# Another order of the pieces on all engines of a four-layer sequence kernel, in the repeated turn and in a lead-up two turns longer

## The chip, the cores and the metric

The kernel runs on one core of one Trainium2 chip. The metric is the time of one execution on the device, in microseconds; lower is better. Three executions of the kernel before took 4561.04 to 4562.57 us, with a median of 4562.22 us.

## The reference

Input x has 32 batches of 256 positions with 256 features. Four layers follow one another, each with a residual; cut to what matters, and without biases and norm weights:

```python
# layer 0 (16 heads) and layer 3 (8 heads): linear attention
q = softmax(norm(x) @ Wq, over the features of a head)
k = softmax(norm(x) @ Wk, over the positions)
y = q @ (k.T @ v)
x = x + silu(norm(y) * (1 + scale(cond)) + shift(cond)) @ Wo
# layer 1 (16 heads): full softmax attention
y = softmax(q @ k.T, over the keys) @ v           # then as above
# layer 2: conditioned selective scan, E = 512, N = 16, once forward and once backward
delta = softplus(u @ Wdbc @ Wdt)
h[t]  = exp(delta[t] * A) * h[t-1] + delta[t] * B[t] * u[t]     # (E, N) numbers per position
y[t]  = sum over N of h[t] * C[t]  +  u[t] * Dp
x = x + gate * ((silu(mx) * (y_forward + y_backward)) @ Wf + skip)
```

## The kernel before, in words

`bass_kernel` (L1610) allocates everything, sets up the weights of layers 0, 1 and 3 (`setup_weights`, L1042), and then starts one instruction stream on each engine with `program` (L1519). The kernel is a software pipeline over the 32 batches: while one batch is in the scans, later ones are in layers 0 and 1 and in the front of layer 2, and an earlier one is in layer 3.

The work of an engine is cut into strands, one for each letter, and each strand is a generator whose `yield`s cut it into pieces. Between the pieces of one strand the order is fixed; between strands it is set by tables of letters alone. `program` runs the pieces in the order of `FIRST[engine]` (L1481, the lead-up), and then repeats `TURN[engine]` (L1497, the repeated turn, one batch of every strand); a letter whose strand is over is skipped. Every wait is written in the piece that needs it, so the tables decide only how early or late a piece stands, and what is queued behind it when it waits. The letters:

- W: weights of the scan layer, made once (on DVE `w_dve`, L1286, lines L1295 to L1371).
- L: layer 0. On DVE the maxima of q and k (L245 to L251), the reciprocals (L254 to L261), y (L265) and the new x (L279); on POOL the product L342.
- A: layer 1. On DVE eight reductions over the scores (`A_sm`, L428; m0 to m7 here), the reciprocal L433, the new x (L279); on POOL the product L484.
- C: the front of layer 2. POOL does m1 and m2 (L656, L659). For each of the two directions DVE makes the delta, `C_dd`, from two inputs in SBUF (L572; d0 and d1 here), POOL multiplies it into delta times u (L663, du0 and du1, which waits for d0 or d1) and writes a column that stops the carry (L665). The result goes to DRAM and comes back as `S_slot`. L668 is the gate.
- S: the scans. A batch has 32 units in 4 columns of 8: four of the forward direction, then four of the backward one. For each unit POOL makes the product with B (L758, S0 to S31), ACT the exponentials in two halves (L699), DVE two scans (L714, S0.0, S0.1 and so on), and PE sums over the states (L793).
- P: the product of the scanned states with C. Units 1, 3, ... 29 have it on POOL (L771, P1, P3, ...), the others on DVE in two halves (L729, P0.0, P0.1, ...).
- G: the gating on DVE (L741), once in a column.
- T: layer 3, with the projection that closes layer 2. It runs the lines of L, and in front of them L821 (`T.gated`) and L824 (`T.x`, which has two inputs in SBUF and makes the x that layer 3 starts from).

Two rings bound how far the engines may part. The exponentials and scans use three PSUM banks, so the exponential of a half waits for what frees the bank three halves before (the scan where P is on POOL, P where it is on DVE). The products with B use eight buffers, so S of a unit on POOL waits for the sum of the unit eight before.

```python
            if i == 0:
                v.wait_ge(S.b.sem, S.b.at(b, "%d" % u))
            v.wait_ge(S.exp.sem, S.exp.at(b, "%d_%d" % (u, i)))
```

```python
        g.wait_ge(S.dve.sem, S.dve.at(b, "d%d" % s))
        g.tensor_tensor(B["dd"][:, :, 1, :], B["dd"][:, :, 1, :], B["dd"][:, :, 0, :], ALU.mult).then_inc(S.pool.sem, 1)
```

The first of these is the start of a scan half (L710 to L712), the second du0 and du1 (L662, L663).

Of the kernel before, what the change touches and what calls it, by code (L numbers as in the profile page):

```python
# [1479 lines left out]

FIRST = {  # L1481
    "PE": (
        "WWWWWWWWWWWWWWWLLLLWLWWWWWLWWLWWWWWWWWWWWWWLWWWWWWLWWWWWWWWWWWWWLAAAAAAAAAAAAAAAAAAAAAAAAAALALLLALLLLLLAAAAAAACACACACACA"
        "ACAAAAACAAAACAACAACCLALLCLALLLLLCLSASAAAAASACSASCACSACACAACASSASASSASSACASASAACASSSACASASCSSCSSSLALSLSCLALSLSSLSSLSLCSSS"
        "LSTASAAAAASACSASCACSATC"),
    "DVE": (
        "WWWWLWWWWWWWWWWWWWWWLWLWWWWLWLWWWWWWWWWWWWWWWWWLWWWWWWWWWWWWWWLWLWWWWWWWWWWWWWWWWWWWWWWWLWAWWWAAAAAAAAAAALLLLLLLLALACCAA"
        "AAAAAACAAALLLLLLCLLASPSLPASSSCPSPSSCSPSSPASASASPASPASASPASASSPGSCPSPSSSPSPSSSSPPSSSPSPSSSSPPSSGSSAPAPSASLSPSSPSLLSSPLSPS"
        "SSLPSPGSSSPSLPC"),
    "ACT": (  # L1490
        "LLLWLLLLLLLLLLAAAAAAAAAAAAAAAAAAALLAAALALLLLLLLLLLAACAAACAACCCCCCCACCAAAACAAACAAACCALLACAALALLLLLCCCCLLLLLSSCSCSCCSASACA"
        "SSSASASCAASCSSCCSSCCSSSSCCACSCSSASSASSASSASSCASASSSASCASSSASSSACSSCSSALSLSACSASALSASLSSSLLSSLSLSCCCCSSSS"),
    "Pool": "LALCCCACSLSSSCPCCSSPSSPSSSSPSSPCSPSSSSPPSSSSSPPPSSSPSSAPSPSC",
    "SP": "LAWWALACCCACLssCCACssCSSCASCLSStSssCCACss",
}
# [177 lines left out]
```

## Time and profile before

| what | value |
|---|---|
| median of 3 executions | 4562.22 us (4561.04 to 4562.57) |
| profiled execution, its span | 4567.5 us |
| DVE busy | 4075.3 us, 89% of the span |
| POOL busy | 3933.3 us, 86% |
| PE busy | 3809.5 us, 83% |
| ACT busy | 3679.7 us, 81% |

The profiled execution is one of its own, beside the three that were timed; of it the span alone is known, which is 5.3 us (0.12%) above their median. Times inside the trace count from the start of that span. A busy share is a mean over the lead-up, some 28 turns alike, and the end, so it does not say which engine sets the length of a turn; that is read from one turn.

### The profile page before, as it was taken

The page shows a single profiled execution, that of the slowest core. Times are in us where ns is not written, and L with a number is a line of the kernel's source. Part 1 is how long each engine was busy: PE and PEld are TensorE (multiplying, and loading weights), DVE is VectorE, ACT ScalarE, POOL GpSimd, SP SyncE. Part 2 cuts the span into 40 slices and gives each one's busy share as a digit, 9 for nine tenths or more (in the row PEclk, how much of TensorE's full clock was granted, in tenths as well). Part 3 has the DMA queues.
Part 4 walks back from the last instruction along what each step waited for, and adds up shares of the span by engine and source line. Part 5 has one row for each costly group of instructions (what it writes and reads, how often), then busy time and mean ns, then how long its engine had stood idle before and what let it go on. Part 6 is the DMA issues. An engine that isn't in the chain of part 4 may idle for free.

```text
span 4567.5 us, 73193 instructions
## 1 busy us (share of the span) xinstructions
PE 3809.5 (83%) x26068; PEld 2509.1 (55%) x26068; DVE 4075.3 (89%) x5552; ACT 3679.7 (81%) x8678; POOL 3933.3 (86%) x1836
## 2 busy tenths in 40 slices
...
GB/s 124 1 8 63 86 108 114 114 116 104 125 115 116 104 97 116 116 116 109 111 118 120 110 93 112 116 112 117 104 124 115 116 103 101 117 113 113 113 108 36
DMA packets 338584, 470.58 MB, mean 103 GB/s; under 512 B 56474, under 2 KB 166149, under 8 KB 338217
## 3 DMA queue, kind: packets, MB, share of 16 engines
...
## 4 chain that ended last, share of the span: by engine, by line
ACT 28%; DVE 22%; POOL 21%; PE 21%; issue 6%; DMA 1%; SPq 1%; DVEq 0%; POOLq 0%; ACTq 0%
POOL S_X L758 13%; ACT ps L699 11%; PE ps L170 8%; POOL S_X L771 6%; DVE S_X L714 5%; PE ps L375 5%; DVE ps L714 5%; DVE A_sm L428 4%; DVE S_X L729 3%; PE ps L394 2%; PE ps L793 2%; PE ps L160 1%; POOL C_dd L663 1%; ACT wa L633 1%; ACT A_ring L153 1%
## 5 line engine op out<-in xcount | busy, mean ns | idle before, releaser
L758 POOL TENSOR_TENSOR S_X<-S_slot,S_bc 128x1024 f32<-128x1024 f32 x1024 | 2398.3, 2368 | 18.6 <-PE ps L793 9.4
L699 ACT ACTIVATE ps<-S_slot,acol 128x256 f32<-128x256 f32 x4096 | 1728.2, 468 | 203.3 <-DVE S_X L729 192.9
L714 DVE TENSOR_TENSOR_SCAN ps<-ps,S_X 128x512 f32<-128x512 f32 x1088 | 1301.1, 1214 | 26.2 <-ACT ps L699 16.0
L714 DVE TENSOR_TENSOR_SCAN S_X<-ps,S_X 128x512 f32<-128x512 f32 x960 | 1138.0, 1206 | 28.5 <-ACT ps L699 26.6
L771 POOL TENSOR_TENSOR S_X<-S_X,S_bc 128x1024 f32<-128x1024 f32 x480 | 1133.4, 2366 | 34.1 <-DVE S_X L714 32.0
L729 DVE TENSOR_TENSOR S_X<-ps,S_bc 128x512 f32<-128x512 f32 x1088 | 723.5, 672 | 10.4
L793 PE MATMUL ps<-S_X,sum 128*32 128x256 f32 x8192 | 621.2, 406 | 83.7 <-POOL S_X L771 73.2
L394 PE MATMUL ps<-A_qP,A_kP 32*128 32x256 f32 x2048 | 318.0, 431 | 123.8 <-ACT A_ring L471 64.1
L793 PEld LDWEIGHTS ps<-S_X,sum 128*32 128x32 f32 x8192 | 201.3, 112 | 371.4 <-issue 175.2
L428 DVE TENSOR_REDUCE A_sm<-ps 128x4 f32<-128x1024 f32 x256 | 312.2, 1220 | 91.0 <-PE ps L375 81.0
L375 PE MATMUL ps<-A_kP,A_qP 32*128 32x256 f32 x2048 | 301.3, 413 | 46.9 <-DVE A_sm L428 26.2
L394 PEld LDWEIGHTS ps<-A_qP,A_kP 32*128 32x128 f32 x2048 | 191.0, 198 | 229.4 <-ACT A_ring L471 105.5
L471 ACT ACTIVATE A_ring<-ps 128x1024 f32<-128x1024 f32 x256 | 259.0, 1012 | 49.7 <-PE ps L394 49.6
L170 PE MATMUL ps<-C_xT,wcz 128*128 128x256 f32 x1024 | 289.8, 433 | 1.0 <-ACT C_dd L609 0.9
L342 POOL TENSOR_TENSOR T_ke<-T_ke,T_xh 128x512 f32<-128x512 f32 x64 | 82.2, 1284 | 233.7 <-ACT T_xh L335 233.7
L663 POOL TENSOR_TENSOR C_dd<-C_dd 128x1024 f32<-128x1024 f32 x64 | 150.9, 2359 | 144.4 <-DVE C_dd L572 144.4
L375 PEld LDWEIGHTS ps<-A_kP,A_qP 32*128 32x128 f32 x2048 | 180.6, 190 | 164.3 <-DVE A_sm L428 91.7
L160 PE MATMUL ps<-ident,T_q 128*128 128x128 f32 x512 | 108.8, 349 | 167.5 <-ACT T_q L153 161.3
L170 PEld LDWEIGHTS ps<-C_xT,wcz 128*128 128x128 f32 x1024 | 214.1, 220 | 57.5 <-issue 24.9
L160 PEld LDWEIGHTS ps<-ident,T_q 128*128 128x128 f32 x512 | 69.4, 172 | 217.7 <-ACT T_q L153 177.3
L484 POOL TENSOR_TENSOR A_ring<-A_ring 128x512 f32<-128x512 f32 x32 | 40.9, 1279 | 170.4 <-ACT A_ring L335 170.4
L785 PE MATMUL ps<-C_xT,wD 128*128 128x256 f32 x512 | 147.7, 413 | 40.7 <-DVE S_g L741 39.8
...
## 6 DMA issues: line engine op xcount, KB each, us to landing
S_slot<-scr_dd SPq DMA_DIRECT2D x1024, 256.0 KB, 4.6
...
S_bc<-scr_bc SPq DMA_DIRECT2D x256, 256.0 KB, 6.3
...
```

The costliest lines, as they stand in the source:

```text
L160: ins = p.transpose(bank[:, col * 256 + r * P:col * 256 + (r + 1) * P], src[:, r, col * P:(col + 1) * P], ident[:])
L170: ins = p.matmul(out, l, r, start=n == 0, stop=n == len(terms) - 1)
L375: ins = p.matmul(bank[o][:, t * 256:(t + 1) * 256], B["qP"][r, g, t * P:(t + 1) * P], B["kP"][r, g, :], start=True, stop=True, tile_positi ...
L394: ins = p.matmul(bank[o][:, t * 256:(t + 1) * 256], B["kP"][r, g, t * P:(t + 1) * P], B["qP"][r, g, :], start=True, stop=True, tile_positi ...
L428: v.tensor_reduce(B["sm"][:, :, 2 * n:2 * n + 2].rearrange("p t h -> p h t"), B["pair"].rearrange("p h (t m) -> p h t m", t=TT), AX, ALU.m ...
L471: a.activation(B["ring"][:, 2 * (n % 4):2 * (n % 4) + 2, :], B["pair"], ACT.Exp).then_inc(S.act.sem, 1)
L699: ins = a.activation(B["bank"][half_at(b, u, i)][:, n * T:(n + 1) * T], B["slot"][:, s, j, 0, :], ACT.Exp, scale=K.k["acol"][:, s, LINES * ...
L714: v.tensor_tensor_scan(line(x if u in ON_POOL else decay), line(decay), line(x), 0.0, ALU.mult, ALU.add).then_inc(S.scan.sem, 1)
L729: v.tensor_tensor(B["X"][:, u % RING, 2 * i:2 * i + 2, :], state, rep(B["bc"][:, s, NQ + q, :], 1, 2), ALU.mult).then_inc(S.cv.sem, 1)
L758: g.tensor_tensor(B["X"][:, u % RING], B["slot"][:, s, :, 1, :], rep(B["bc"][:, s, q, :], 1, LINES), ALU.mult).then_inc(S.b.sem, 1)
L771: g.tensor_tensor(B["X"][:, u % RING], B["X"][:, u % RING], rep(B["bc"][:, s, NQ + q, :], 1, LINES), ALU.mult).then_inc(S.cp.sem, 1)
L793: ins = p.matmul(B["sums"][32 * j:32 * j + 32, (c % 2) * T:(c % 2 + 1) * T], K.k["sum4"][:], B["X"][:, u % RING, j, :], start=False, stop= ...
```

## The change

The tables `FIRST` and `TURN` are written anew for all five engines. Each `TURN` holds as many pieces of every letter as before. Each `FIRST` is longer by exactly two turns' pieces (on DVE 533 letters for 255, on POOL 170 for 60), so the pipeline stands at the same depth where the repeated turn begins. No instruction, wait, buffer or size changes. The lines behind the tables have numbers higher by 14. Of the diff the tables of POOL stand for all:

```diff
 FIRST = {
...
-    "Pool": "LALCCCACSLSSSCPCCSSPSSPSSSSPSSPCSPSSSSPPSSSSSPPPSSSPSSAPSPSC",
...
+    "Pool": (
+        "LALCCCSSSCPSALSSSSCSCCPSPPSSSSSSPPSCPSSSPSSPPSSPSPSSSSPSPSSAPCSLSSPSSSPCSCCSPSSSPSSSPPSSSCPSPSSSSPSTSSPPPSSSSPSPSCSP"
+        "SSASLSCPSSCCSPSSSSSPPPSSSPSPSSSCPSSSSPSTPPSSSPSSSPCAPS"
+    ),
...
 TURN = {
...
-    "Pool": "SPSLSSSCPCCSSPSSPSSSSPSSPCSPSSSSPPSSSSSPTPPSSSPSSAPSPSC",
...
+    "Pool": "SPSLSSSCPCCSSPSPSSSSSSPSPSSCSPPSSPSSSPSTSPSSPSPSAPSSPSC",
```

**POOL, second column of the scans.** Before, with S8 to S11, P7, S12, S13, P9, then du0 and its column (L663, L665), then S14 and P11:

```order
L758 TENSOR_TENSOR S_X<-S_slot,S_bc 128x1024 x4
L771 TENSOR_TENSOR S_X<-S_X,S_bc 128x1024
L758 TENSOR_TENSOR S_X<-S_slot,S_bc 128x1024 x2
L771 TENSOR_TENSOR S_X<-S_X,S_bc 128x1024
L663 TENSOR_TENSOR C_dd<-C_dd 128x4x256
L665 MEMSET C_dd 128x4
L758 TENSOR_TENSOR S_X<-S_slot,S_bc 128x1024
L771 TENSOR_TENSOR S_X<-S_X,S_bc 128x1024
```

Now, with S7 to S12, P7, S13, P9, then S14 and S15, and du0 behind them:

```order
L758 TENSOR_TENSOR S_X<-S_slot,S_bc 128x1024 x6
L771 TENSOR_TENSOR S_X<-S_X,S_bc 128x1024
L758 TENSOR_TENSOR S_X<-S_slot,S_bc 128x1024
L771 TENSOR_TENSOR S_X<-S_X,S_bc 128x1024
L758 TENSOR_TENSOR S_X<-S_slot,S_bc 128x1024 x2
L663 TENSOR_TENSOR C_dd<-C_dd 128x4x256
L665 MEMSET C_dd 128x4
```

Two products with B that stood behind du0 now stand between P9 and du0.

**DVE, the same place.** Before, from S9.0 and S9.1 to P10.1; d0 is L572, T's maximum of k is L251:

```order
L714 SCALAR_TENSOR_TENSOR S_X<-ps,S_X 128x512 x2
L729 TENSOR_TENSOR S_X<-ps,S_bc 128x512
L251 TENSOR_REDUCE T_km<-ps 128x2
L741 SCALAR_TENSOR_TENSOR S_g<-ps,bD,wa 128x256
L714 SCALAR_TENSOR_TENSOR ps<-ps,S_X 128x512
L572 SCALAR_TENSOR_TENSOR C_dd<-C_dd,C_tmp 128x4x256
L729 TENSOR_TENSOR S_X<-ps,S_bc 128x512
L714 SCALAR_TENSOR_TENSOR ps<-ps,S_X 128x512
L729 TENSOR_TENSOR S_X<-ps,S_bc 128x512
```

Now, from P8.1 ahead of S9.0 to P10.1:

```order
L729 TENSOR_TENSOR S_X<-ps,S_bc 128x512
L714 SCALAR_TENSOR_TENSOR S_X<-ps,S_X 128x512 x2
L714 SCALAR_TENSOR_TENSOR ps<-ps,S_X 128x512
L741 SCALAR_TENSOR_TENSOR S_g<-ps,bD,wa 128x256
L729 TENSOR_TENSOR S_X<-ps,S_bc 128x512
L714 SCALAR_TENSOR_TENSOR ps<-ps,S_X 128x512
L572 SCALAR_TENSOR_TENSOR C_dd<-C_dd,C_tmp 128x4x256
L251 TENSOR_REDUCE T_km<-ps 128x2
L729 TENSOR_TENSOR S_X<-ps,S_bc 128x512
```

P8.1 moved ahead of S9.0, S10.1 and P10.0 ahead of d0, the maximum of k behind it; and P10.1 no longer follows at once on the scan whose result it reads.

**DVE in the lead-up.** Before, around the end of batch 0's layer 1 and the start of batch 1's layer 0, with none of the W work left:

```order
L433 RECIPROCAL A_srec<-ps 128x32
L436 TENSOR_TENSOR A_qP<-ps,A_srec 128x512
L135 BN_STATS A_raw<-A_qP 128x6 x2
L138 BN_AGGR A_mv<-A_raw 128x2 x2
L135 BN_STATS T_raw<-L_xin 128x6 x2
L138 BN_AGGR T_mv<-T_raw 128x2 x2
L245 TENSOR_REDUCE T_qm<-ps 128x32
```

Now batch 1's layer 0 is at its end while W's pieces (L1295 to L1299) still run between its own:

```order
L259 SCALAR_TENSOR_TENSOR T_bd<-ps,same 128x128 x2
L261 RECIPROCAL T_qm<-ps 128x32
L1299 COPY wdt<-ps 64x512
L1297 TENSOR_SCALAR wcz<-ps,S_bc 128x512
L265 TENSOR_TENSOR T_q<-ps,T_qm 128x512
L135 BN_STATS T_raw<-T_q 128x6 x2
L138 BN_AGGR T_mv<-T_raw 128x2 x2
L1297 TENSOR_SCALAR wcz<-ps,S_bc 128x512
L1299 COPY S_slot<-ps 128x256 x3
L279 TENSOR_TENSOR A_x<-ps,A_x 128x512
L279 TENSOR_TENSOR A_x<-ps,L_xin 128x512
```

Layer 0 of batch 1 moved from behind the W work to between its pieces, and with it the start of batch 1's layer 1.

## Rows read from the trace of the kernel before

**Rows 1.** The page's first part: busy time, share of the span, instructions.
```profile
PE 3809.5 (83%) x26068; PEld 2509.1 (55%) x26068; DVE 4075.3 (89%) x5552; ACT 3679.7 (81%) x8678; POOL 3933.3 (86%) x1836
```
**Rows 2.** Stretches: us, busy PE, PEld, DVE, ACT, POOL, granted clock, DMA share, GB/s.
```profile
200.00:300.00 100.00, 62.47 (x307) 38.70 (x306) 14.93 (x22) 24.48 (x47) 1.26 (x1) 0.62 0.01 3
...
3107.00:3234.00 127.00, 111.38 (x802) 73.87 (x802) 124.25 (x169) 114.42 (x271) 123.03 (x58) 0.96 0.48 112
...
3361.00:3490.00 129.00, 113.75 (x801) 74.78 (x800) 124.36 (x168) 114.55 (x271) 122.64 (x58) 0.93 0.48 111
```
**Rows 3.** The chain that ended last, one mark of each turn: start, us, what.
```profile
2596.20 2.47 ACT ps L699 x6
...
2725.28 2.47 ACT ps L699 x6
...
2852.12 2.47 ACT ps L699 x6
...
4127.90 2.47 ACT ps L699 x6
```
**Rows 4.** Waits of DVE, 600 to 4200 us: total, times, longest.
```profile
DVE S_X L714 <- ACT ps L699: 16.6, 28, 1.9
```
**Rows 5.** Waits of POOL, the same stretch.
```profile
POOL C_dd L663 <- DVE C_dd L572: 80.9, 56, 1.7
```
**Rows 6.** POOL's timeline at du0: start, us, engine, line, [idle before].
```profile
3171.75 4.77 POOL L758 TENSOR_TENSOR S_X<-S_slot,S_bc 128x1024 f32<-128x1024 f32 x2
3177.16 2.36 POOL L771 TENSOR_TENSOR S_X<-S_X,S_bc 128x1024 f32<-128x1024 f32 x1 [0.64 <-DVE S_X L714]
3181.10 2.37 POOL L663 TENSOR_TENSOR C_dd<-C_dd 128x1024 f32<-128x1024 f32 x1 [1.58 <-DVE C_dd L572]
```
**Rows 7.** DVE's timeline of the same turn, from one d1 to the next.
```profile
3119.71 1.23 DVE L572 SCALAR_TENSOR_TENSOR C_dd<-C_dd,C_tmp 128x1024 f32<-128x1024 f32 x1
...
3174.76 2.32 DVE L714 TENSOR_TENSOR_SCAN S_X<-ps,S_X 128x512 f32<-128x512 f32 x2
...
3179.81 1.21 DVE L572 SCALAR_TENSOR_TENSOR C_dd<-C_dd,C_tmp 128x1024 f32<-128x1024 f32 x1
...
3181.53 1.22 DVE L714 TENSOR_TENSOR_SCAN ps<-ps,S_X 128x512 f32<-128x512 f32 x1
3182.79 0.69 DVE L729 TENSOR_TENSOR S_X<-ps,S_bc 128x512 f32<-128x512 f32 x1
...
3246.55 1.22 DVE L572 SCALAR_TENSOR_TENSOR C_dd<-C_dd,C_tmp 128x1024 f32<-128x1024 f32 x1
```
**Rows 8.** DVE's timeline near the end, two L572.
```profile
4264.15 3.98 DVE L572 SCALAR_TENSOR_TENSOR C_dd<-C_dd,C_tmp 128x1024 f32<-128x1024 f32 x1
...
4320.51 5.20 DVE L572 SCALAR_TENSOR_TENSOR C_dd<-C_dd,C_tmp 128x1024 f32<-128x1024 f32 x1
```
**Rows 9.** POOL's timeline beside these two.
```profile
4262.31 2.42 POOL L771 TENSOR_TENSOR S_X<-S_X,S_bc 128x1024 f32<-128x1024 f32 x1
4264.65 2.40 POOL L758 TENSOR_TENSOR S_X<-S_slot,S_bc 128x1024 f32<-128x1024 f32 x1
...
4322.26 2.37 POOL L771 TENSOR_TENSOR S_X<-S_X,S_bc 128x1024 f32<-128x1024 f32 x1
```
**Rows 10.** DVE's timeline at one T.x.
```profile
3014.46 1.03 DVE L824 TENSOR_TENSOR xs<-T_x,T_xh 128x512 f32<-128x512 f32 x1
```
**Rows 11.** POOL's timeline beside it.
```profile
3012.59 2.35 POOL L771 TENSOR_TENSOR S_X<-S_X,S_bc 128x1024 f32<-128x1024 f32 x1
3015.09 1.53 POOL L656 TENSOR_TENSOR xs<-C_xh,C_mod 128x512 f32<-128x512 f32 x1
```
**Rows 12.** DVE's timeline in the lead-up, batch 1 and batch 2 leaving layer 0.
```profile
276.87 0.73 DVE L135 BATCH_NORM_STATS2 T_raw<-L_xin 128x6 f32<-128x256 f32 x2
...
316.75 0.69 DVE L279 TENSOR_TENSOR A_x<-ps,L_xin 128x512 f32<-128x512 f32 x1 [11.57 <-PE ps L170]
...
448.74 0.69 DVE L279 TENSOR_TENSOR A_x<-ps,L_xin 128x512 f32<-128x512 f32 x1 [1.39 <-PE ps L170]
```

More of the change, by code:

```diff
@@ L1482 @@
     "PE": (
-        "WWWWWWWWWWWWWWWLLLLWLWWWWWLWWLWWWWWWWWWWWWWLWWWWWWLWWWWWWWWWWWWWLAAAAAAAAAAAAAAAAAAAAAAAAAALALLLALLLLLLAAAAAAACACACACACA"
-        "ACAAAAACAAAACAACAACCLALLCLALLLLLCLSASAAAAASACSASCACSACACAACASSASASSASSACASASAACASSSACASASCSSCSSSLALSLSCLALSLSSLSSLSLCSSS"
-        "LSTASAAAAASACSASCACSATC"),
-    "DVE": (
-        "WWWWLWWWWWWWWWWWWWWWLWLWWWWLWLWWWWWWWWWWWWWWWWWLWWWWWWWWWWWWWWLWLWWWWWWWWWWWWWWWWWWWWWWWLWAWWWAAAAAAAAAAALLLLLLLLALACCAA"
-        "AAAAAACAAALLLLLLCLLASPSLPASSSCPSPSSCSPSSPASASASPASPASASPASASSPGSCPSPSSSPSPSSSSPPSSSPSPSSSSPPSSGSSAPAPSASLSPSSPSLLSSPLSPS"
-        "SSLPSPGSSSPSLPC"),
@@ L1490 @@
-    "ACT": (
-        "LLLWLLLLLLLLLLAAAAAAAAAAAAAAAAAAALLAAALALLLLLLLLLLAACAAACAACCCCCCCACCAAAACAAACAAACCALLACAALALLLLLCCCCLLLLLSSCSCSCCSASACA"
-        "SSSASASCAASCSSCCSSCCSSSSCCACSCSSASSASSASSASSCASASSSASCASSSASSSACSSCSSALSLSACSASALSASLSSSLLSSLSLSCCCCSSSS"),
-    "Pool": "LALCCCACSLSSSCPCCSSPSSPSSSSPSSPCSPSSSSPPSSSSSPPPSSSPSSAPSPSC",
-    "SP": "LAWWALACCCACLssCCACssCSSCASCLSStSssCCACss",
+        "WWWWWWWWWWLLWLLWWLLWLLWWLWWWWWWLWWAAAAAAWAWAWLAWAWALAWWAWWAAWLWAWAWWWWAALAWWALWALAALAAWLAWWWLWAWLWWWWWAWAAACAACACACA"
@@ new lines @@
+        "CACAALCAAALACACALAACAALACASCALALLCALLSALAAAAAASSASACSASCSCACAACASCSLSAASCLSSSAASASACLAACASSASSASSCSACSASSLLALSSSSLSC"
+        "LASSLSCSLSTAASAAAAATATSSASCSSACSACATSATCTACTACSSASTSASAASSATCASSCSTSAASCATASCLSCLASSLSSCSALSCSLLSSLSLLSSSASLTASAAASA"
+        "TTASACSACACTSSSASCAACATATSACSTSCSASASTAASAASSATACCTASSATSCSSSACLSLLSCLSASLSSLLASSLLCSSSSLTASAAAAASCSASSACTACSAC"
+    ),
+    "DVE": (
+        "WWWWWWWWLWLLWWWWWWLWWWWLWWWWWWWWLWLLWWWWWWWWWWWWWLAWLWWAWAAAWAWWAALWWWLAWWWWWLWWWWLWWWAAALWWLLWWWWALWCWWAWWWWWWWWWCW"
+        "WWALAAAAACAALLLSSPPSLSCAAASPSLPLSLASLASSPPSCSSPLSPSSSCPAASPASSASASAPSGAPSSASPCSLPSSSPSPLSSSPPSSLSSPSPSSGPSSPSSSPPSSS"
+        "SPALAPGSACSSPSSSPSPSPLSSLLSPSSPAPSPCGSPLSASPSSTPTSPSSTSSPASSPACTSATSPPASASSATPSPSSASGASPSPSSSCPPSSSSPSTPSSTSSPPTSTSG"
+        "PSPSSSPSSPSSTLSPSPSSPSPLLASASASGLSPPLSSSCPSPSSLSPLSLSPSPSPPSSGPASSLCPASPSSSPTTTSPSSCSPSTTPSSASSAPSSPATSSAPSAPAGSASPA"
+        "SPSSSSSPPSSCSPTPSSSSPTGPTTSSSPSSPSTSLSPSPASALLSPLASPLSSGCSSPPSSLSPSSP"
+    ),
@@ new lines @@
+    "ACT": (
+        "LLLLLLLLLLLLLAAALAAAALWAAALLAALLALAAALAAAAAALALLLLCAAACACAAACCLCCCCCCALCALCACASAASSALSASCALCCACCLALSLSCASACAACCLALLL"
+        "SLSCASASSASSACASSASACLCSSCCSCSSCSCSCLSCACSSSSASSASASCASSLCSSALSASSSSACSASSACSSSSACCSCSCLSALSSLASSALSSSAASCSLSLLSLSLS"
+        "SCCCSASASSACSSAASTAASCTSSCSCSSSCSTTSSCTSTCSCSASCTCSSCCSASSSASASSSSASSASSCTSASTATSCTTSASSSSACLSCSSLSCASCCSSCLALCSSLSL"
+        "SLSALSSACSSAASCLSSLLSLLSSCCSSSASACSASSATSSTASASCASSCCSSSTSCSSTCSSCTSTSASCSCTSACSSACSASASSASSASACSACTSTTTATSCSSSSACLS"
+        "LCCSCCSSLSLASLLASALSLASACSSSSSSS"
+    ),
@@ L1495 @@
+    "Pool": (
+        "LALCCCSSSCPSALSSSSCSCCPSPPSSSSSSPPSCPSSSPSSPPSSPSPSSSSPSPSSAPCSLSSPSSSPCSCCSPSSSPSSSPPSSSCPSPSSSSPSTSSPPPSSSSPSPSCSP"
+        "SSASLSCPSSCCSPSSSSSPPPSSSPSPSSSCPSSSSPSTPPSSSPSSSPCAPS"
+    ),
+    "SP": "LWAWLAACLCCCAssCCssASCLCSCSACSSCSssCCAtCssSSCASSCSLCSssCTstsACSLCCSSASCSSsstTACCCss",
 }
 TURN = {
-    "PE": "ACATACASSATSASSASSTACTASASTATATCASSSATCASASCSTSCSSSLALSLSCLALSLSSLSSLSLCSSSLSTASAAAAASACSASCACSATC",
+    "PE": "ATACACAASTSSCSASATASASTASTATATCASSSSATCAASCTSCSSASLSLSSCLSSLSALSLSLSLSLCSSSLTASAAAAASCASCASSTACSAC",
```

10 lines of the change are left out of this document (5 added, 5 removed).

## The prediction

> **What bounds the kernel now.** The page's first part shows that no engine is idle for long: DVE is busy 89% of the span, POOL 86%, PE 83%, ACT 81% [rows 1]. Such shares mix the lead-up with the turns, so I went to the table of stretches next. In a turn of 127 us DVE is busy for 124.25 and POOL for 123.03; DVE's spare time is some 2.75 us, POOL's 4 [rows 2]. Between 200 and 300 us it is the reverse: PE is busy for 62 us at a granted clock of 0.62, DVE for 15, and POOL does one instruction [rows 2]. So the kernel has two parts with different limits: a lead-up that waits for one batch to get through layers 0 and 1 on PE, and turns in which DVE and POOL have hardly a gap.
>
> The chain that ended last gives the length of a turn by its mark, six halves of exponentials: from 2596.20 to 4127.90 are 12 turns, 127.64 us each; a quick one takes 126.84 (2725.28 to 2852.12) [rows 3]. The slow turns are ones in which PE's clock falls once more, as in the stretch of 129 us at 0.93 beside that of 127 us at 0.96, with DVE busy for no longer (124.36 for 124.25) [rows 2].
>
> What DVE and POOL wait for tells where the order matters. POOL's largest wait is du0 and du1 for DVE's delta, 80.9 us in 56 waits, 1.4 us each [rows 5]; one of DVE's longest is of a scan for an exponential, 16.6 us in 28, a small sum [rows 4]. The first is a curious one. DVE's timeline has d0 start at 3179.81, the moment at which POOL has gone idle behind P9 (3177.16 + 2.36 = 3179.52) [rows 6, 7]. In a turn d0 and d1 thus fall into an empty POOL, and take 1.2 us. Near the end of the kernel they don't: there two of the same shape take 3.98 and 5.20 us [rows 8]. Beside the first, POOL's P ended at 4264.73, its next S began at 4264.65 in the record and ended at 4267.05, and DVE's instruction ended at 4268.13, 1.08 after that; beside the second, POOL's P ended at 4324.63, DVE at 4325.71, again 1.08 later [rows 8, 9]. **I read from this that DVE's L572 doesn't begin its work until POOL's queued instructions are through**, even where an instruction boundary lies between (4264.65), and that it then takes 1.1 to 1.2 us.
>
> **The change, part by part.** The counts of instructions don't change, so every term is a wait that goes or comes. I follow one turn from d1 to d1; before, d1 to d0 is 60.10 us (3119.71 to 3179.81) and d0 to d1 is 66.74 (to 3246.55), 126.84 in all [rows 7].
>
> *d1 to d0.* S9.1 ended 57.37 us after d1 (3174.76 + 2.32 - 3119.71) [rows 7]. Ahead of it one product more now stands (P8.1), +0.6, the distance of such a product to the next instruction. ACT does two halves of exponentials before the piece of layer 0 on which POOL's chain to S4 hangs: 2.47 / 6 = 0.41 each [rows 3], and as S4 has hardly any lead over its scan I charge +0.4. A scan with its product right behind costs 1.26 us from start to start (3181.53 to 3182.79 [rows 7]) where a scan before an independent instruction costs 1.16 (half of 2.32); ten of eleven such neighbours are parted in the new turn, and one lies in this stretch: -0.2 with what follows on it. Two of A's maxima are asked for earlier: +0.3, between 0 and 0.6. S9.1 then ends at 58.5.
>
> Now the step on which all rests. du0 now stands behind S14 and S15 on POOL. P9 waits for S9.1 as before (0.64 us of idle time [rows 6]), and then P9, S14 and S15 follow without a wait: 2.36 + 4.77 (the size of a pair of such products) = 7.1, less what the records overlap, 7.0 [rows 6]. DVE comes to d0 3.3 us after S9.1 (S10.0, the gating, P10.0, S10.1: 1.13 + 0.4 + 0.6 + 1.13), in the middle of S14. By the reading above it gets through only behind S15: its work starts at 58.5 + 7.0 = 65.5, and not at 61.8. Everything on DVE behind it stands still for 3.7 us, which DVE's 2.75 us of spare time do not cover, since they lie at other places.
>
> *d0 to d1.* Out go S10.1 and P10.0, -1.7; in comes the maximum of k, +0.6. Parted neighbours: -0.8 (seven at 0.1 to 0.13). POOL has T's product one scan unit earlier and a sum at S23 in time: -0.7, at most what DVE waits in a turn, 2.75, at least 0. That is 66.74 - 2.6 = 64.1. The maximum of k is 3.3 us later than before, and with it ACT's exponentials of layer 3's k, which lie between those of the scans: 0 to +1.0, I take +0.3. The turn becomes 65.5 + 64.4 = 129.9, +3.1 over the quick one; bounds +2.3 and +4. There are 28 turns in which d0 meets running scans (batches 4 to 31): **+87 us** (+64 to +112).
>
> *The lead-up.* Before, batch 1's layer 0 begins only after batch 0's layer 1 (276.87), and ends 40 us later (316.75) [rows 12], on an idle DVE. Now it is made between W's pieces, on a PE that W alone doesn't fill. I laid the new order of PE, ACT and DVE out with durations of the trace: batch 1's layer 1 starts at about 252 us (240 to 290), not 317. Batch 2 leaves layer 0 at 448.74 before [rows 12]; in the new order at about 374, 75 sooner, and with six scan halves more behind it, at 127.6 / 64 = 2.0 us each: 75 + 12 = 87, less some for their waits, 82. But in the lead-up too, L572 and L824 now fall beside a full POOL; by the same reading seven of them lose 1 to 4.7 us, 20 in all. **-62 us** (-90 to -40).
>
> *Nothing.* SP's new order moves loads that are needed tens of us later, with the same slots; at nothing, under the cover of the DMA engines' 48% share [rows 2]; if a slot came late, its S would wait, first on POOL. The end of the kernel drains in the same letters.
>
> **The sum.** 4567.5 + 87 - 62 = 4592.5 for a profiled span; less the 5.3 us by which that stands above the median, **4587 us**, +0.5%.
>
> **The rivals.**
>
> *DVE gets through at the next boundary.* At one L824, issued at 3014.46 beside P (3012.59 + 2.35 = 3014.94), the end was 3015.49, 0.55 after P's, and POOL's next, L656, took 1.53 [rows 10, 11]. So a boundary can be enough; but L656 waits for several semaphores, S15 for one. If it held for d0, it would start at S14's end, 58.5 + 4.7 = 63.2: a turn of 127.6, with POOL held up once +0.6 to +0.8 over the quick one; 28 x 0.6 = +17, the lead-up -72: 4562 - 55 = 4507. SBUF — State Buffer, of the Trainium skill, section "Who interferes with whom", states the rule that an instruction of DVE with two inputs in SBUF contends with GpSimd's reads, and that the order of issue decides who blocks for a whole instruction. By that rule this rival would be right, and the case below wrong; the trace agrees with the contention (3.98 and 5.20 us [rows 8]), but in the first of those POOL had two instructions in turn.
>
> *There is no such block.* The long L572 near the end would then have another cause, such as its own input. d0 starts at 61.8, the turn is 61.8 + 64.1 = 125.9, -0.9; 28 x -0.9 = -26, the lead-up -82: 4454. Against it: both long ones end 1.08 us behind a POOL instruction.
>
> *The block, and a lead-up that gives little* (the W pieces in turn delay layer 1 on PE), with T late for its full microsecond: 28 x 3.6 = +100, -40: 4622.
>
> *The block, and PE's clock falls once more in every turn*, since PE stands still with DVE: the slow turn before 2725.28 took 129.08 us, 2.2 over the quick one, where the mean is 0.8 over it [rows 3]; 28 x 1.4 = +40: 4627.
>
> **How the numbers follow.** My case has 0.50, the boundary 0.14, no block 0.12, the weak lead-up 0.14, the clock 0.10. About 0.2% (9 us) can be told from no change, so same is 4553 to 4571. Within my case the bounds of the turn (+64) and the lead-up (-90) reach 4536, and 0.06 of its 0.50 lie under 4553, 0.12 in between. Faster: 0.14 + 0.12 + 0.06 = 0.32. Same: 0.12. Slower: 0.32 + 0.14 + 0.10 = 0.56. The range leaves out the case without a block and a tail above the weak lead-up (4562 + 112 - 40 = 4634 at its bounds): 4495 to 4635. My case's own range is 4536 to 4634.
>
> **What would show it.** In the changed profile d0 (L572 at the second column) should last 4.5 to 4.9 us in each turn, d1 1.2; du0's wait for DVE, 1.6 us, should stay, behind S15; the marks of the chain should lie 129 to 131 us apart; the first L714 should stand near 370. d0 at 2.5 us and turns of 127.5 speak for the boundary, d0 at 1.2 for no block, and then I am wrong by over 1%. First L714 past 410 would break the lead-up's term.

## The result, and the profile after

The changed kernel takes 4579.09 us (median of 11 runs, 4565.88 to 4598.32), where the kernel before, in the same runs, takes 4562.22 us (4557.94 to 4571.9): 1.0041 times, 95% interval 1.0027 to 1.0056. It is slower by 17 us, where +25 was forecast. Its profiled execution has a span of 4589.5 us, 10 us above that median, so the trace shows a turn somewhat longer than the median execution has.

The first part of its page:

```profile
PE 3816.3 (83%) x26068; PEld 2500.9 (54%) x26068; DVE 4114.0 (90%) x5552; ACT 3667.2 (80%) x8678; POOL 3968.6 (86%) x1836
```

The shares are those of [rows 1]. DVE is busy for 39 us more and POOL for 35. On DVE the longer time is that of two lines alone: all L572 together last 139.5 us for 85.0, all L824 43.6 for 31.5, and no other line changes by 2 us. Both have two inputs in SBUF. (That is 67 us; busy time rises by less, since it counts once where two records overlap, and they overlap more in the new order.) On POOL the products with B (L758) last 26 us longer. Read beside the timelines below, this is time in which one engine stands in the way of the other. The table of stretches, to be read beside [rows 2]:

```profile
200.00:300.00 100.00, 88.56 (x491) 61.55 (x490) 31.51 (x65) 43.83 (x94) 7.84 (x6) 0.86 0.12 33
...
2304.00:2434.00 130.00, 112.91 (x808) 74.35 (x808) 125.00 (x169) 114.42 (x272) 124.38 (x58) 0.95 0.48 110
2434.00:2567.00 133.00, 115.10 (x805) 75.05 (x801) 126.92 (x168) 114.14 (x272) 124.14 (x58) 0.92 0.46 107
2567.00:2702.00 135.00, 117.55 (x808) 76.46 (x805) 127.13 (x169) 114.39 (x272) 124.98 (x58) 0.91 0.45 106
```

Between 200 and 300 us PE now is busy for 89 us at a granted clock of 0.86, where it was 62 at 0.62: the lead-up no longer waits for one batch. The turns are 130 to 135 us, and the long ones are those with the lower clock.

Where the time came from and went is told by the d1 of single batches (L572 on DVE, the second of each batch). Batch 4 and batch 31 in the changed kernel:

```profile
872.19 2.56 DVE L572 SCALAR_TENSOR_TENSOR C_dd<-C_dd,C_tmp 128x1024 f32<-128x1024 f32 x1
...
4400.52 2.37 DVE L572 SCALAR_TENSOR_TENSOR C_dd<-C_dd,C_tmp 128x1024 f32<-128x1024 f32 x1 [0.21 <-ACT C_tmp L625]
```

and in the kernel before:

```profile
949.84 1.23 DVE L572 SCALAR_TENSOR_TENSOR C_dd<-C_dd,C_tmp 128x1024 f32<-128x1024 f32 x1
...
4390.31 1.41 DVE L572 SCALAR_TENSOR_TENSOR C_dd<-C_dd,C_tmp 128x1024 f32<-128x1024 f32 x1
```

| part | before | after | difference |
|---|---|---|---|
| start to d1 of batch 4 | 949.8 | 872.2 | -77.7 |
| 27 turns, d1 of batch 4 to batch 31 | 3440.5 | 3528.3 | +87.9 |
| from there to the end | 177.2 | 189.0 | +11.8 |
| span | 4567.5 | 4589.5 | +22.0 |

That is 3.25 us for each of the 27 turns (the 22 us between the two profiled spans stand beside the 17 between the medians). DVE's waits between 600 and 4200 us, and then POOL's, beside [rows 4, 5] (us in total, times, longest):

```profile
DVE A_sm L428 <- PE ps L375: 41.6, 84, 2.4
DVE S_g L741 <- PE ps L793: 37.5, 31, 1.9
```

```profile
POOL S_X L758 <- PE ps L793: 54.1, 33, 3.2
...
POOL C_dd L663 <- DVE C_dd L572: 32.5, 28, 1.2
```

du0's wait for d0 is gone: the 28 waits that are left are those of du1. A new one has come, of POOL's product with B for a sum of PE. One turn shows how. PE's timeline at layer 1's last score product and its maxima:

```profile
2230.29 1.28 PE L375 MATMUL ps<-A_kP,A_qP 32*128 32x256 f32 x8
2232.90 0.39 PE L381 MATMUL ps<-ident,A_sm 128*16 128x128 f32 x2 [1.33 <-DVE A_sm L428]
2233.22 0.64 PE L793 MATMUL ps<-S_X,sum 128*32 128x256 f32 x8
```

DVE's:

```profile
2231.62 1.23 DVE L428 TENSOR_REDUCE A_sm<-ps 128x4 f32<-128x1024 f32 x1 [1.66 <-PE ps L375]
...
2238.75 0.48 DVE L741 SCALAR_TENSOR_TENSOR S_g<-ps,bD,wa 128x256 f32<-128x256 f32 x1 [1.94 <-PE ps L793]
...
2240.88 1.21 DVE L572 SCALAR_TENSOR_TENSOR C_dd<-C_dd,C_tmp 128x1024 f32<-128x1024 f32 x1
```

POOL's, with P7, S13, P9, the pair S14 and S15, and du0:

```profile
2228.96 2.34 POOL L771 TENSOR_TENSOR S_X<-S_X,S_bc 128x1024 f32<-128x1024 f32 x1
2233.97 2.36 POOL L758 TENSOR_TENSOR S_X<-S_slot,S_bc 128x1024 f32<-128x1024 f32 x1 [2.67 <-PE ps L793]
2236.28 2.37 POOL L771 TENSOR_TENSOR S_X<-S_X,S_bc 128x1024 f32<-128x1024 f32 x1
2238.60 5.69 POOL L758 TENSOR_TENSOR S_X<-S_slot,S_bc 128x1024 f32<-128x1024 f32 x2
2244.25 2.35 POOL L663 TENSOR_TENSOR C_dd<-C_dd 128x1024 f32<-128x1024 f32 x1
```

Two things are to be seen. PE's L381 waits for DVE's last maximum, and the sum of unit 5 (2233.22), which the new order puts behind it, comes late for POOL's S13, which stands idle for 2.67 us. And d0 starts at 2240.88, the moment at which S14 ends, takes 1.21 us, and it is POOL's S15 that is held up: the pair takes 5.69 us, where such a pair took 4.77 [rows 6]. d0 did not wait until POOL was through. Over batches 4 to 31 d0 lasts 1.2 us ten times, 1.5 to 1.8 eight times, 2.8 to 2.9 nine times and 2.55 once, and never the 4.5 to 4.9 that were forecast.

d1, for which 1.2 us were forecast, is held up too. DVE's and POOL's timelines at one of them:

```profile
2434.34 2.54 DVE L572 SCALAR_TENSOR_TENSOR C_dd<-C_dd,C_tmp 128x1024 f32<-128x1024 f32 x1
```

```profile
2433.43 2.36 POOL L758 TENSOR_TENSOR S_X<-S_slot,S_bc 128x1024 f32<-128x1024 f32 x1
2436.95 2.35 POOL L663 TENSOR_TENSOR C_dd<-C_dd 128x1024 f32<-128x1024 f32 x1 [1.16 <-DVE C_dd L572]
```

DVE now asks for d1 while POOL's last product in front of du1 runs, and d1 ends 1.09 us behind it. In the repeated turns of every kernel here with the new turn, whichever steps of it are undone below, d1 lasts 2.0 to 2.7 us; in all kernels with the old turn it lasts 1.2 to 1.3. In the changed kernel that is 33 us of DVE's time in 27 turns. No run takes it away, so what it costs the turn was not measured.

### The profile page after: what moved, and what is told of

It is laid out like the page before. It is cut to its first block, busy times and chain, and to the rows that moved or that the text cites. A ratio compares the mean times of both kernels' runs of the same rounds, so it can differ in the third digit from the quotient of the medians.

```text
span 4589.5 us, 73193 instructions
## 1 busy us (share of the span) xinstructions
PE 3816.3 (83%) x26068; PEld 2500.9 (54%) x26068; DVE 4114.0 (90%) x5552; ACT 3667.2 (80%) x8678; POOL 3968.6 (86%) x1836
## 4 chain that ended last, share of the span: by engine, by line
PE 37%; DVE 26%; ACT 21%; issue 8%; POOL 5%; DMA 1%; SPq 0%; DVEq 0%; POOLq 0%; ACTq 0%
PE ps L170 21%; ACT ps L699 8%; DVE ps L714 7%; DVE S_X L714 7%; PE ps L375 4%; DVE A_sm L428 4%; ACT A_ring L471 4%; PE ps L793 3%; DVE S_X L729 3%; POOL S_X L758 3%; PE ps L394 2%; PE ps L160 2%; ACT T_q L153 1%; POOL S_X L771 1%; ACT T_ke L325 1%
## 5 line engine op out<-in xcount | busy, mean ns | idle before, releaser
L758 POOL TENSOR_TENSOR S_X<-S_slot,S_bc 128x1024 f32<-128x1024 f32 x1024 | 2430.3, 2393 | 101.8 <-PE ps L793 61.3
L793 PE MATMUL ps<-S_X,sum 128*32 128x256 f32 x8192 | 633.2, 408 | 107.0 <-POOL S_X L771 93.9
L394 PE MATMUL ps<-A_qP,A_kP 32*128 32x256 f32 x2048 | 313.9, 427 | 44.2 <-ACT A_ring L471 39.4
L471 ACT ACTIVATE A_ring<-ps 128x1024 f32<-128x1024 f32 x256 | 260.1, 1016 | 94.3 <-PE ps L394 92.7
L170 PE MATMUL ps<-C_xT,wcz 128*128 128x256 f32 x1024 | 272.7, 413 | 3.1 <-ACT C_dd L609 2.8
L394 PEld LDWEIGHTS ps<-A_qP,A_kP 32*128 32x128 f32 x2048 | 187.9, 198 | 154.5 <-ACT A_ring L471 89.0
L160 PE MATMUL ps<-ident,T_q 128*128 128x128 f32 x512 | 99.6, 326 | 196.7 <-ACT T_q L153 190.9
L170 PEld LDWEIGHTS ps<-C_xT,wcz 128*128 128x128 f32 x1024 | 198.1, 204 | 66.2 <-issue 34.7
L663 POOL TENSOR_TENSOR C_dd<-C_dd 128x1024 f32<-128x1024 f32 x64 | 150.4, 2350 | 79.7 <-DVE C_dd L572 79.7
L609 ACT ACTIVATE C_dd<-ps,bdt 128x256 f32<-128x256 f32 x256 | 106.3, 467 | 141.1 <-PE ps L538 141.1
L538 PE MATMUL ps<-C_dbc,wdt 64*128 64x256 f32 x512 | 148.2, 411 | 41.2 <-ACT C_dd L615 41.1
```

Source lines behind the costliest of these rows:

```text
L160: ins = p.transpose(bank[:, col * 256 + r * P:col * 256 + (r + 1) * P], src[:, r, col * P:(col + 1) * P], ident[:])
L170: ins = p.matmul(out, l, r, start=n == 0, stop=n == len(terms) - 1)
L394: ins = p.matmul(bank[o][:, t * 256:(t + 1) * 256], B["kP"][r, g, t * P:(t + 1) * P], B["qP"][r, g, :], start=True, stop=True, tile_positi ...
L471: a.activation(B["ring"][:, 2 * (n % 4):2 * (n % 4) + 2, :], B["pair"], ACT.Exp).then_inc(S.act.sem, 1)
L758: g.tensor_tensor(B["X"][:, u % RING], B["slot"][:, s, :, 1, :], rep(B["bc"][:, s, q, :], 1, LINES), ALU.mult).then_inc(S.b.sem, 1)
L793: ins = p.matmul(B["sums"][32 * j:32 * j + 32, (c % 2) * T:(c % 2 + 1) * T], K.k["sum4"][:], B["X"][:, u % RING, j, :], start=False, stop= ...
```

## The experiments

Eleven variants, in four groups. All times are medians, and each ratio is to the kernel before in the same runs. That kernel's median lay between 4562 and 4571 us from one set of runs to the next, so a difference between variants of different sets is good to some 8 us, unless it is taken over the ratios.

**The lead-up and the turn apart.** Both tables come whole from one kernel and whole from the other, which is possible since the pipeline stands at the same depth where the turn begins.

```diff
 # the changed kernel, with TURN of before (first) or with FIRST of before (second)
-TURN = {...}     # changed
+TURN = {...}     # before
...
-FIRST = {...}    # changed
+FIRST = {...}    # before
```

> The lead-up of the change with the repeated turn of before. In the changed kernel's trace batch 4 passes d1 78 us earlier than before (872.19 for 949.84 us), and each later turn loses 3.2. If lead-up and turn are independent, the 78 us stay and turns are 127.6 us: 4562 - 78 = 4484. If the gain of the lead-up only exists because the engines stand further apart than the old turn lets them (so that the first turns give it back), it is 4520 or more. The last two turns inside the new lead-up already have the new order's waits and cost some 6 us of it in both.

> The lead-up of before with the repeated turn of the change. Independent parts: every turn from the end of the old lead-up 3.2 us longer, 28 to 30 times, and 12 us more in the drain at the end, where the changed kernel took 189.0 us behind its last d1 for 177.2: 4562 + 94 + 12 = 4668. If the loss in the turns comes from the state that the new lead-up leaves behind, and not from the turn's order, under 4600.

The new lead-up with the old turn takes 4505.11 us, ratio 0.9863 (0.9847 to 0.9879): 60 us faster, and the fastest kernel of this study. The old lead-up with the new turn takes 4660.54 us, 1.0207 (1.0185 to 1.0229): 96 us slower. The signs of the two halves are settled: the lead-up gains, the turn loses. In the first of the two the d1 of batches 4 and 31 are:

```profile
886.45 1.25 DVE L572 SCALAR_TENSOR_TENSOR C_dd<-C_dd,C_tmp 128x1024 f32<-128x1024 f32 x1
...
4327.36 1.40 DVE L572 SCALAR_TENSOR_TENSOR C_dd<-C_dd,C_tmp 128x1024 f32<-128x1024 f32 x1
```

63 us ahead of the kernel before, at both: the 27 turns between take 3440.9 us, as before (3440.5). Of the 78 us that the lead-up had gained where the new turn follows, 14 were given back where the old one takes over. The expectation, 4484, was too low by 21 us: by these 14, by the 3 that the kernel before took more here (4565.02), and by 4 that stay open.

**One step of the change in the kernel before.** First POOL's alone, du0 behind S14 and S15 (S15 comes in front of P11 by it too):

```diff
-    "Pool": "SPSLSSSCPCCSSPSSPSSSSPSSPCSPSSSSPPSSSSSPTPPSSSPSSAPSPSC",
+    "Pool": "SPSLSSSCPCCSSPSSPSSSSPSSPSSCPSSSPPSSSSSPTPPSSSPSSAPSPSC",
```

> The kernel before with one step of the change on POOL alone: in the repeated turn the products for units 14 and 15 stand in front of du0. DVE reaches d0 2.7 us behind S9.1, during the first of them. If d0 has to wait until POOL's queue is through (the prediction), it lasts 5.5 us in each turn and 28 x 4 = 112 us are added: 4675. If it gets in at the next boundary of POOL's instructions, it lasts 3.2 us, POOL's second product is held up by 1.1, and 28 x (1 to 2) are added: 4590 to 4620. If there is no contention d0 stays at 1.2 and the time at 4562.

4627.3 us, 1.0142 (1.0126 to 1.0157). DVE's d0 and POOL's pair and du0 in one of its turns:

```profile
2562.05 3.11 DVE L572 SCALAR_TENSOR_TENSOR C_dd<-C_dd,C_tmp 128x1024 f32<-128x1024 f32 x1
```

```profile
2561.71 5.66 POOL L758 TENSOR_TENSOR S_X<-S_slot,S_bc 128x1024 f32<-128x1024 f32 x2
2567.34 2.35 POOL L663 TENSOR_TENSOR C_dd<-C_dd 128x1024 f32<-128x1024 f32 x1
```

d0 is asked for beside S14, lasts 3.11 us and ends at 2565.16, 1.1 us behind the end of S14 (2561.71 + 2.35); S15 is held up by 1.0. It gets in at the next boundary of POOL's instructions: not the block to the end of the queue that I had read, but the first rival. The price is +2.1 us a turn (129.7 for 127.6), 64 in all, which is just above the 2 that were the upper end for the boundary. Near the end of the same kernel it is otherwise again:

```profile
4371.27 9.72 DVE L572 SCALAR_TENSOR_TENSOR C_dd<-C_dd,C_tmp 128x1024 f32<-128x1024 f32 x1
```

```profile
4372.97 2.33 POOL L771 TENSOR_TENSOR S_X<-S_X,S_bc 128x1024 f32<-128x1024 f32 x1
4375.26 4.63 POOL L758 TENSOR_TENSOR S_X<-S_slot,S_bc 128x1024 f32<-128x1024 f32 x2
```

Here d0 ends at 4380.99, 1.1 us behind POOL's last queued product (4379.89), with three boundaries, at 4372.97, 4375.26 and inside the pair, gone by. So neither reading holds everywhere: in the turns the boundary lets d0 in, near the end it often does not.

Second PE's step alone, L381 in front of the sums of units 5 and 6:

```diff
-    "PE": "ACATACASSATSASSASSTACTASASTATATCASSSATCASASCSTSCSSSLALSLSCLALSLSSLSSLSLCSSSLSTASAAAAASACSASCACSATC",
+    "PE": "ACATACAASSTSASSASSTACTASASTATATCASSSATCASASCSTSCSSSLALSLSCLALSLSSLSSLSLCSSSLSTASAAAAASACSASCACSATC",
```

> The kernel before with one step of the change on PE alone: in the repeated turn the transposes of layer 1's maxima (L381), which wait for DVE's last maximum, stand in front of the sums of units 5 and 6. Theory PE: POOL then waits in each turn for the sum of unit 5, 1 to 2.7 us, and 28 times 1 to 2.5 are added: 4590 to 4630. If the wait is covered (POOL in this order asks for the sum of unit 5 one instruction earlier, but DVE's last maximum comes earlier too), under 4575.

4605.07 us, 1.0092 (1.0072 to 1.0112), +41. The wait is there in each turn, as in this one (PE's timeline, then POOL's):

```profile
2555.57 0.39 PE L381 MATMUL ps<-ident,A_sm 128*16 128x128 f32 x2 [1.42 <-DVE A_sm L428]
2555.88 1.07 PE L793 MATMUL ps<-S_X,sum 128*32 128x256 f32 x16
```

```profile
2556.63 2.36 POOL L758 TENSOR_TENSOR S_X<-S_slot,S_bc 128x1024 f32<-128x1024 f32 x1 [1.84 <-PE ps L793]
```

Both steps together (the two diffs above):

> The kernel before with both single steps of the change: on POOL the products for units 14 and 15 in front of du0 (alone +62 us), on PE L381 in front of the sums of units 5 and 6 (alone +41). If the two losses add, 4562 + 103 = 4665, the whole of what the new turn costs with the old lead-up (+96 us). If they cover each other, since both hold POOL and DVE at the same place of the turn, 4625 to 4640.

4614.39 us, 1.0103 (1.0082 to 1.0125): 43 us over before, less than the first step costs alone. The losses do not add. What the trace shows is that POOL waits for the sum in each turn here too, and that d0 now lasts 1.21 to 2.53 us instead of 3.1; that the one brings the other, by shifting POOL's queue against DVE, is a reading. And together they are not the whole: the new turn costs 96 with this lead-up, so more than half of it is not accounted for by these two. Two things that the other moves bring are in the traces and were not tried apart: d1's 2.0 to 2.7 us, which this kernel does not have (1.2 to 1.3), and the time that PE spends at the lower clock, of which more below.

**Steps undone in the changed kernel.** PE's step undone:

```diff
-    "PE": "ATACACAASTSSCSASATASASTASTATATCASSSSATCAASCTSCSSASLSLSSCLSSLSALSLSLSLSLCSSSLTASAAAAASCASCASSTACSAC",
+    "PE": "ATACACASSATSCSASATASASTASTATATCASSSSATCAASCTSCSSASLSLSSCLSSLSALSLSLSLSLCSSSLTASAAAAASCASCASSTACSAC",
```

> The changed kernel with one thing undone on PE in the repeated turn: the sums of units 5 and 6 stand in front of the transposes of layer 1's maxima (L381) again. Theory PE: POOL's product for unit 13 waits 2.67 us for the sum of unit 5, which stands on PE behind L381, which waits for DVE's last maximum; that is the turn's main loss, the wait goes under 0.5 us, turns shrink by 2 to 2.7 us, and the time is 4579 - 26 x 2.3 = 4520. Theory POOL (the prediction's): the loss comes from products with B queued in front of du0, and the turn keeps at least 129.3 us: 4570 or more; then with POOL free earlier, d0 should show as 3.5 us long in every turn instead of 1.2.

POOL's step undone:

```diff
-    "Pool": "SPSLSSSCPCCSSPSPSSSSSSPSPSSCSPPSSPSSSPSTSPSSPSPSAPSSPSC",
+    "Pool": "SPSLSSSCPCCSSPSPSSSSSSPSPCSSSPPSSPSSSPSTSPSSPSPSAPSSPSC",
```

> The changed kernel with one thing undone on POOL in the repeated turn: du0 (L663) stands directly behind P9 again, in front of the products for units 14 and 15. Theory POOL (the prediction's): d0 never waits for POOL again, turns shrink by over 2 us, to under 128.5, 4579 - 26 x 2.6 = 4511. Theory PE: d0 already begins at an instruction boundary of POOL in most turns (1.21 us in 12 of 27, up to 2.86 in the others), so at most 1 us a turn comes back: 4555 to 4579, and POOL's wait of 2.7 us for the sum of unit 5 stays.

The first takes 4549.39 us, 0.9961 (0.9948 to 0.9975), the second 4550.91 us, 0.9965 (0.9954 to 0.9975): 28 to 30 us less than the changed kernel, each. In the first POOL's wait for sums falls from 54.1 to 5.8 us, turns are 127.3 to 130.8, and d0 lasts 2.7 us in each. In the second nearly every turn is 129.7 us long and d0 takes 1.21, but du0 waits up to 3.5 us, 124.0 us in 55 waits, since DVE comes to d0 only behind S10.1. Each step gave part of the time back, and neither all that its theory had promised.

Both undone:

> The changed kernel with both steps undone: PE's sums of units 5 and 6 in front of L381, and POOL's du0 directly behind P9. Alone they gave -30 and -28 us. If the two losses are separate they add: 4579 - 58 = 4521. If they cover each other (either of them sets the turn), the second gives little more: 4540 to 4550. DVE still reaches d0 only behind S10.1, so POOL keeps a wait of up to 3.5 us at du0.

4626.04 us, 1.0127 (1.009 to 1.0164): not faster than one alone, but 77 us slower. Neither theory held. The trace shows where the time is. Between batches 4 and 29 fifteen of its turns take 129.7 to 130.8 us and ten take 134.7 to 136.2, with the same instructions, and d0 lasts 1.2 in all of them. The same place of a short turn and of the long one behind it, as stretches (the columns are those of [rows 2]), and DVE's wait, 600 to 4200 us:

```profile
2666.00:2683.00 17.00, 14.65 (x139) 10.22 (x138) 15.99 (x23) 16.90 (x40) 17.00 (x9) 1.00 0.36 84
2796.00:2813.00 17.00, 17.00 (x86) 11.34 (x84) 8.85 (x16) 9.98 (x24) 13.08 (x7) 0.50 0.29 64
```

```profile
DVE S_g L741 <- PE ps L793: 38.1, 10, 3.8
```

In the long turn PE's granted clock goes to the lower of its two levels (1.2 GHz, half of full speed) at 2796, after PE had waited 1.5 us for a product of POOL. For 17 us PE is busy throughout and makes 86 matmuls, where it made 139. The waits come behind that: POOL stands idle for 3.9 us for a sum up to 2809.27, DVE for 3.8 up to 2811.72, once in each of the ten long turns. So most of what this kernel loses is PE at half speed: ten turns that are 5.7 us longer make 57 us. Why the clock falls at this place in some turns and not in others is not shown; in the short turn PE waits as long there (1.46 us), and it does not fall.

And with d0 directly behind S10.0 on DVE as well:

```diff
-    "DVE": "LSLSAPSSPSPPSGPSLPACSSSTPSTPSSCTSSPSPASASAPSASPASSAPTATSAPSSSGPSCTPSSSSPTSPSSSPPSSTSPTSTSGPSSSPPSSSAPSAPSATLSSSPPSSSLPLSSPLGSSLSPPSSSSPSLPC",
+    "DVE": "LSLSAPSSPSPPSGPSLPACSSSTPSTPSSCTSSPSPASASAPSASPASSAPTATSAPSSSCGPSTPSSSSPTSPSSSPPSSTSPTSTSGPSSSPPSSSAPSAPSATLSSSPPSSSLPLSSPLGSSLSPPSSSSPSLPC",
```

> As a_both, and on DVE d0 stands directly behind the scan S10.0 again, in front of P10.0 and S10.1. POOL's wait at du0 goes from 3.5 to about 1.6 us; if POOL's time sets the turn, 26 x 1.5 = 40 us less than a_both, and turns of 126 to 127.5 us: 4480 to 4500, which would say that the rest of the new turn is as good as the old one. If PE, DVE or layer 1's chain sets it, no more than 10 us less than a_both.

4657.69 us, 1.0205 (1.019 to 1.022): the changed kernel with three of its steps taken back is 79 us slower than with all of them. Its trace shows what the rest of the new order has to do with them. PE's timeline, then ACT's:

```profile
2536.32 2.04 PE L785 MATMUL ps<-C_xT,wD 128*128 128x256 f32 x4 [2.94 <-DVE S_g L741]
2538.29 2.08 PE L394 MATMUL ps<-A_qP,A_kP 32*128 32x256 f32 x8
```

```profile
2540.42 1.02 ACT L471 ACTIVATE A_ring<-ps 128x1024 f32<-128x1024 f32 x1 [2.74 <-PE ps L394]
```

The new order has the third column's D product (L785) in front of layer 1's second score product (L394). It waits for DVE's gating, 2.94 us; behind it L394 comes late, behind that ACT's L471, and behind L471 the scans' exponentials, for which DVE then waits (136.6 us in 110 waits, 600 to 4200 us). After its wait PE runs at half its speed, 2.08 us for eight products that take 1.13 elsewhere; the granted clock of that stretch is 0.55:

```profile
2535.00:2546.00 11.00, 9.57 (x34) 5.62 (x35) 8.12 (x10) 5.96 (x14) 8.61 (x5) 0.55 0.69 188
```

So a fourth step was undone, on PE alone. It moves two pieces: the D product (L785) behind the first of layer 1's score products that follow, and C's projection for the second direction (L170) behind the third:

```diff
-    "PE": "ATACACASSATSCSASATASASTASTATATCASSSSATCAASCTSCSSASLSLSSCLSSLSALSLSLSLSLCSSSLTASAAAAASCASCASSTACSAC",
+    "PE": "ATACACASSATSASSATACSASTASTATATCASSSSATCAASCTSCSSASLSLSSCLSSLSALSLSLSLSLCSSSLTASAAAAASCASCASSTACSAC",
```

> As a_three, and on PE also the fourth step undone: C's projection for the second direction and the third column's D product (L785), which waits up to 2.9 us there for DVE's gating, stand behind the first two products of layer 1's scores (L394) again. Theory: in a_three PE waits for the gating, layer 1's exponentials (L471, 135 us of waits for L394) wait for PE, and the scans' exponentials are queued behind them on ACT; PE then falls to half its clock. Undone, these waits go and the turn comes to 127.6 us or less: 4505 or less, the time of the new lead-up with the old turn. If the falls of the clock have another cause, the turn stays over 130 and the time over 4580.

4562.46 us, 0.9985 (0.9973 to 0.9997), 95 us less than a_three, and less than the changed kernel. PE's waits at L785 for the gating fall from 105.0 to 60.3 us, ACT's at L471 for L394 from 135.0 to 49.9, and DVE's for exponentials from 136.6 to 59.8. So the chain L785, L394, L471, exponential is borne out, with two reserves: two pieces moved at once, and the clock moved with them (see the table at the end). The expectation of 4505 was not reached: most turns alternate between 127.8 and 131.6 us, with mean granted clocks of 0.96 and 0.94, so what is left of the loss lies in moves that were not taken apart.

**The prediction's gain by itself.** Scans parted from the products that read them, in the fastest kernel (new lead-up, old turn), on DVE alone; seven instructions move by a place or two:

```diff
-    "DVE": "LSLSAPSSPSPPSGPSLPASSSCPSTTTPSSCSPSSPASASASPASPASASTPATSASSPTGSCPSPSSSPSPTSSSSPPSSTSPTTSPSSSSPPSSGSSAPAPSASTLSPSSPSLLSSPLSPSSSLPSPGSSSPSLPC",
+    "DVE": "LSLSAPSSPSPPSGPSLPASSSCPSTTTPSSCSSPSPASASASPASPASASTPATSASSPTGSCPSSPSSSPTSPSSSPPSSTSPTSTSPSSSPPSSGSSAPAPSASTLSSPSPSLLSSPLSPSSSLPSPGSSSPSLPC",
```

> The new lead-up with the old turn (4505 us), and on DVE alone seven instructions moved by one place, so that a scan is no longer followed at once by the product that reads it (P4.0, P10.1, P12.0, P12.1, P16.1, P22.0 and the statistics of layer 3's y). Prediction's term: each such pair costs 0.1 to 0.13 us of DVE's time; if DVE's time is the turn, 7 x 0.115 x 26 = 21 us less, 4484. If POOL or PE's clock sets the turn, or if an exponential waits longer because its bank comes free later, 4500 to 4510.

4572.52 us, 1.0015 (0.9998 to 1.0033): 67 us slower than without it (61, with each set against the kernel before in its own runs), where 21 less were expected. POOL's waits for scans in this kernel, and those of DVE for exponentials:

```profile
POOL S_X L771 <- DVE S_X L714: 84.0, 62, 7.0
```

```profile
DVE ps L714 <- ACT ps L699: 53.5, 80, 1.3
```

The first was 44.8 us in 39 waits in the kernel with the pairs together, the second 2.2 us in 10. My reading: a product that is moved behind the next scan frees its PSUM bank one scan later, 1.1 us; the exponential that waits for the bank comes later by as much, and ACT has no slack for it: DVE wins a tenth of a microsecond and waits for 0.7 (53.5 / 80). The 51 us more of these waits are near the loss of 61; a run that moves one pair alone was not made.

## Why the prediction was right, and where it was not

The measured 4579 lies 8 us from the forecast of 4587, inside its range, on the side that was given 0.56. The two large terms were right in size: the lead-up -62 (measured -78 at batch 4, -63 with the old turn behind it), the turns +87 (measured +88). But the mechanism on which the second rested, a d0 blocked for 4.5 to 4.9 us in each turn, did not happen. Its size was luck, so this is taken point by point.

- *What bounds the kernel.* Right: a lead-up limited by one batch's way through PE, and turns without gaps. Both halves were shown by swapping the tables.
- *The lead-up.* The working was good in its order and cautious in its numbers. Layer 0 of batch 1 was put at 252 us and comes at 245.62; that of batch 2 at 374, and it comes at 347.96; the first scan "near 370" at 307.75. The 20 us that L572 and L824 were to lose there came to some 9 (the excess over their times before, up to batch 3's d1).

```profile
245.62 0.69 DVE L279 TENSOR_TENSOR A_x<-ps,L_xin 128x512 f32<-128x512 f32 x1 [2.29 <-PE ps L170]
...
307.75 1.23 DVE L714 TENSOR_TENSOR_SCAN ps<-ps,S_X 128x512 f32<-128x512 f32 x1 [2.96 <-POOL S_X L758]
...
347.96 0.69 DVE L279 TENSOR_TENSOR A_x<-ps,L_xin 128x512 f32<-128x512 f32 x1 [1.61 <-PE ps L170]
```

- *"DVE's L572 doesn't begin its work until POOL's queued instructions are through."* This is the step that failed. It came from two rows near the end [rows 8], and in the turns it does not hold: d0 gets in at the next boundary, at the latest (2.86 us at most in the changed kernel, 3.11 in b_du0_late), as L824 did at 3014.46 [rows 10], which I had set aside because the POOL instruction behind it waits for several semaphores. The row nearest in kind to the place was that one. The SBUF — State Buffer page of the Trainium skill, section "Who interferes with whom", says that a DVE instruction with two inputs in SBUF contends with GpSimd's reads and that the order of issue decides who blocks; d0's 3.11 us beside S14 agree with it, its 9.72 us beside four instructions do not. The rival with the boundary was the right mechanism for d0, and had 0.14; its time of 4507 was 72 us off.
- *The sum of du0's move.* 3.7 us of standing DVE were charged. Done alone it costs 2.1 a turn, of which DVE's own standing still is 1.9 (3.11 - 1.21). In the changed kernel d0 stands still for 0.7 us in the mean. The rival's +0.6 to +0.8 was too low, as it had set the gains of parted neighbours against the block.
- *"d1 1.2."* It lasts 2.0 to 2.7 us in the turns, some 1.2 more than before. No term stood for that, and no run undoes it.
- *PE's order.* No term at all stood for it, though the order of all engines changed, and I had read only DVE's and POOL's closely. L381 in front of the sums of units 5 and 6 costs 41 us alone. "du0's wait for DVE should stay": it went, since POOL comes later than DVE.
- *Parted neighbours, -1.0 a turn.* The pitch difference is real (1.26 and 1.13 us), and it is in the changed kernel's trace: in one turn the short gaps of 0.03 us between DVE's instructions fall from ten to four. But the cost of what comes later behind a moved product was left out. In the old turn seven such moves lose 61 to 67 us in all, so there the term has the wrong sign; in the new turn it was not tried.
- *The clock.* The rival with one fall more in a turn (0.10) is in part what happened, in eight of the 27 turns: those of 132.9 to 135.0 us go with mean clocks of 0.91 to 0.92, the others up to batch 29, of 127.8 to 130.0, with 0.95 to 0.96. The eight are also the turns in which d0 lasts 2.85 us. It is counted in the +88 and not beside it.
- *There is no such block.* This rival's turn was added up as 61.8 + 64.1, where the main case has 64.4 for the second part: with the same figure it is 126.2, -0.6, and 4463 instead of 4454. It did not happen either way.
- *The end of the kernel*, costed at nothing: +11.8 in the trace. Of it 4 us are one T.x (L824), which lasts 5.59 us at 4423.55 where the same one took 1.51 before. Which part of the order does the rest was not tried apart; with the old lead-up and the new turn it is 181.3 us from the last d1 to the end, with the new lead-up and the old turn 176.6.

So the forecast held by luck: a charge for d0 that was too large stood in for three that were missing, PE's order, d1 and the clock. How the +88 divides among them is not shown. The runs that undo one step at a time would not have shown this alone: a_pe_max and a_pool_du0 gave back 30 us each, which reads like two halves of a cause, and a_both then took 77 away, most of it by PE's clock.
